# Cross attention added to 32 batches: slots of two adjacent rows, queries tile by tile

## The reference

```python
def _L0_xattn_ref(tgt, memory, Wq, Wk, Wv):      # tgt, memory: 32 x 512 x 512 f32
    NH = 16                                      # dk = 32
    q = (tgt @ Wq.T)...; k = (memory @ Wk.T)...; v = (memory @ Wv.T)...
    scores = jnp.einsum('bhqd,bhkd->bhqk', q, k) * scale
    probs = jax.nn.softmax(scores, axis=-1)
    att = jnp.einsum('bhqk,bhkd->bhqd', probs, v)
    tgt2 = att[0]
    return tgt + tgt2
```

## Time and profile before

| what | us |
|---|---|
| median of 3 runs | 198.37 (197.28 to 200.08) |
| the profiled execution | 198.03 |
| its span | 195.8 |
| PE busy | 129.3 (66%) |
| DVE busy | 103.1 (53%) |
| ACT busy | 92.6 (47%) |
| POOL busy | 84.0 (43%) |
| moved by DMA | 71.49 MB, mean 365 GB/s |

### The profile page before, as it was taken

The page is one execution under the profiler, slowest core; times in us unless marked ns, Lnnn a source line. Parts: engine busy times, 40 slices in busy tenths (PEclk is TensorE's granted clock), DMA queues, the critical chain, the costliest instruction groups (busy, mean ns, idle before and its releaser), DMA issues.

```text
span 195.8 us, 3210 instructions
## 1 busy us (share of the span) xinstructions
PE 129.3 (66%) x1213; PEld 95.6 (49%) x1213; DVE 103.1 (53%) x165; ACT 92.6 (47%) x221; POOL 84.0 (43%) x39
## 2 busy tenths in 40 slices
PE   6799999999898978989789897889720000000000
PEld 6788878878665655666556665556510000000000
DVE  0645565208454999759897598974279800000000
ACT  2624553202788958888598886988800000000000
POOL 1000000000000699999999999998059920000000
PEclk9999999999999999999999999999995555555555
DMA  6999999999998099999999999999999999999995
GB/s 208 331 397 387 385 387 386 387 386 385 388 386 305 24 338 343 340 340 270 390 396 389 387 403 409 403 408 403 406 393 388 408 408 409 409 409 408 408 388 210
DMA packets 40701, 71.49 MB, mean 365 GB/s; under 512 B 1264, under 2 KB 10480, under 8 KB 40688
## 3 DMA queue, kind: packets, MB, share of 16 engines
q1 hardware_dynamic: 40688, 71.31, 98.8%
HBM read 37.75 MB, written 33.55 MB: 364 GB/s over the span
## 4 chain that ended last, share of the span: by engine, by line
PE 38%; ACT 15%; DVE 11%; issue 5%; POOL 5%; DMA 3%; POOLq 2%; SPq 0%; ACTq 0%; DVEq 0%
PE bank L309 17%; ACT probs L420 9%; PE bank L367 7%; PE bank L333 6%; ACT probs_t L414 5%; PE bank L346 5%; POOL ring L272 5%; DVE neg_max L453 4%; DVE ring L492 3%; DMA x_first<-in_x_dram 3%; PE bank L322 3%; POOLq L55 2%; DVE x_first L492 2%; PE bank L357 1%; DVE att_t L463 1%
## 5 line engine op out<-in xcount | busy, mean ns | idle before, releaser
L272 POOL TENSOR_TENSOR ring<-ring,att 128x1024 f32 (+1 forms) x33 | 83.3, 2565 | 72.9 <-DVE att L476 72.9
L453 DVE TENSOR_REDUCE neg_max<-bank 128x1 f32<-128x512 f32 x64 | 41.6, 679 | 16.2 <-PE bank L333 16.2
L420 ACT ACTIVATE probs<-bank,neg_max 128x512 f32<-128x512 f32 x64 | 45.3, 709 | 8.4 <-DVE neg_max L453 8.3
L414 ACT COPY probs_t<-bank 128x512 f32<-128x512 f32 x64 | 37.8, 595 | 17.8 <-PE bank L367 17.7
L367 PE MATMUL bank<-ident,probs 128*128 128x128 f32 x256 | 39.0, 282 | 6.6 <-ACT probs L420 6.3
L367 PEld LDWEIGHTS bank<-ident,probs 128*128 128x128 f32 x256 | 27.4, 140 | 21.5 <-ACT probs L420 20.8
L333 PE MATMUL bank<-k_t,q_t 32*128 32x512 f32 x192 | 29.9, 424 | 0.0
L492 DVE TENSOR_TENSOR ring<-ring,bank 128x1024 f32<-128x1024 f32 (+1 forms) x16 | 23.2, 1478 | 0.6 <-DMA ring<-in_x_dram 0.6
L333 PEld LDWEIGHTS bank<-k_t,q_t 32*128 32x128 f32 x192 | 15.0, 183 | 7.1 <-issue 5.7
L346 PE MATMUL bank<-probs_t,v 128*32 128x128 f32 x512 | 17.3, 276 | 0.7 <-ACT probs_t L414 0.7
L346 PEld LDWEIGHTS bank<-probs_t,v 128*32 128x32 f32 x512 | 13.0, 109 | 4.0 <-ACT probs_t L414 4.0
(11 more groups left out here) (33 smaller groups left out, 72.1 us busy)
## 6 DMA issues: line engine op xcount, KB each, us to landing
ring<-in_x_dram SPq DMA_DIRECT2D x28, 1024.0 KB, 13.7
out_dram<-ring SPq DMA_DIRECT2D x21, 1024.0 KB, 13.4
out_dram<-ring SPq DMA_DIRECT2D x14, 512.0 KB, 6.1
x_first<-in_x_dram SPq DMA_DIRECT2D x4, 768.0 KB, 13.9
out_dram<-x_first SPq DMA_DIRECT2D x3, 1024.0 KB, 14.2
...
wk_raw<-in_L_xattn_Wk_dram SPq DMA_DIRECT2D x1, 1024.0 KB, 9.2
```

Of the source, the lines that this page charges most:

```text
L272: nc.gpsimd.tensor_tensor(xs, xs, a.unsqueeze(1).to_broadcast([P, BPG, a.shape[1]]), ALU.add).then_inc((tail_added if tail else added)[g], 1)
L414: nc.scalar.copy(probs_t[:, h % PT_SLOTS, :, :], bank[:, PT_BANK + h % 2, :].rearrange("p (t n) -> p t n", t=T)).then_inc(probs_t_ready, 1)
L420: nc.scalar.activation(probs[:, h % 2, :], bank[:, h % S_BANKS, :], ACT.Exp, bias=neg_max[:, h:h + 1], scale=1.0, accum_out=row_sum[:, h:h ...
L453: nc.vector.tensor_reduce(neg_max[:, h:h + 1], bank[:, h % S_BANKS, :], AX_X, ALU.max, negate=True).then_inc(max_ready, 1)
```

## The change

- Rows 2p and 2p + 1 of a half (256 rows) lie on partition p. A tile is now one of these rows of each partition: tiles 0 and 1 are the two rows of the first half, tiles 2 and 3 of the second. A slot holds two batches, both rows (1 MB, runs of 4 KB). There are 16 groups and 17 slots; `x_first` is gone. The order of the keys is changed likewise, which the sum over keys doesn't see.
- Queries are projected per tile, x as the stationary operand: x is turned, multiplied with wq (12 matmuls), scaled to `q_raw` by ACT, turned again and split by ACT and DVE. Tile 0's queries are made first, tile 1's during tile 0's heads, those of tiles 2 and 3 after the turn back of the tile before. The heads of tile 0 are interleaved with the products of keys and values, in an order written out for each engine.
- `heads(j)` issues no scores of the next tile; the first two pairs are issued ahead of it by `score_pair`. All tiles are turned back and normalised whole.
- Tiles 0 and 1 are added and stored by rows of slots (512 KB, rows of 2 KB), 9 groups by DVE and 7 by POOL, 1024 elements a partition each. The second half is added and stored by whole slots after tile 3, 11 by DVE and 5 by POOL, 2048 elements each.
- In `heads` DVE puts an add ahead of every maximum from head 0 on while any are left: eight in tile 1, five in tile 2, none in tile 3.
- SP loads slots when the operand that lies there is used up: slot 7 after the turns of wq, 8 and 9 after those of wk, 10 after those of wv, 11 and 12 after the keys, 13 to 16 after the last values.
- ACT's order in tile 0, not shown: exponents run up to three heads ahead of the copies, and `copy_transposed(0, h)` waits from h = 6 on until the group that used its place in `probs_t` is weighed.

```diff
-BPG = 4
+BPS = 2
+ROWS = 2
...
+    S_BANKS = 4
+    PT_BANK, BACK_BANK, ATT_T_BANK = 4, 6, 7
+    PT_SLOTS = 6
+    POOL_GROUPS = (1, 3, 5, 7, 10, 12, 14)
+    DVE_GROUPS = (0, 2, 4, 6, 8, 9, 11, 13, 15)
+    WHOLE_POOL_GROUPS = (2, 5, 8, 11, 14)
+    WHOLE_DVE_GROUPS = (0, 1, 3, 4, 6, 7, 9, 10, 12, 13, 15)
+    LAST_HALF = T // ROWS - 1
...
-    x_rows = x.rearrange("b (j p) d -> p j b d", p=P)
-    out_rows = out.rearrange("b (j p) d -> p j b d", p=P)
+    x_rows = x.rearrange("b (j p r) d -> p j b r d", p=P, r=ROWS)
+    out_rows = out.rearrange("b (j p r) d -> p j b r d", p=P, r=ROWS)
...
-        x_first = sb("x_first", [P, T, BPG, D])
...
+        WQ_RAW, WK_RAW, CTX_RAW, WV_RAW, WK_T, CTX_T, WV_T = 7, 8, 9, 10, 11, 13, 15
...
+        slots = sb("slots", [P, SLOTS, BPS, ROWS, D])
...
+        x0_q = sb("x0_q", [P, 2, C, 2, P], F32R)
...
+        att_rows = sb("att_rows", [P, ROWS, D])
+        att, q_raw = att_rows[:, 0, :], att_rows[:, 1, :]
...
+        JOBS = [("x0_t", 0, 0), ("wq_t", 0, 1), ("wq_t", 1, 2), ("wq_t", 2, 3), ("wq_t", 3, 4), ("q", 0, 5),
+                ("wk_t", 0, 6), ("ctx_t", 0, 7), ("q_t", 0, 0), ("ctx_t", 1, 1), ("ctx_t", 2, 2), ("ctx_t", 3, 3),
+                ("k_t", 0, 4), ("wk_t", 1, 5), ("k_t", 1, 6), ("wk_t", 2, 7), ("wk_t", 3, 4), ("wv_t", 0, 5),
+                ("k_t", 2, 6), ("wv_t", 1, 7), ("wv_t", 2, 7), ("k_t", 3, 6), ("wv_t", 3, 7),
+                ("x0_t", 1, 6), ("v", 0, 7), ("v", 1, 6), ("v", 2, 7), ("v", 3, 6),
+                ("q", 1, 6), ("q_t", 1, 0)]
+        for j in range(2, T):
...
+        def slot_of(J, g):
+            return g if J == 0 else (g - 1) % SLOTS
...
+            def load(J, g):
+                sp.dma_start(slots[:, slot_of(J, g), :, :, :], x_rows[:, J, 2 * g:2 * g + 2, :, :]).then_inc(
+                    loaded[J][g], 16)
+            def store_row(r, g):
+                sp.wait_ge(added[g], r + 1)
+                sp.dma_start(out_rows[:, 0, 2 * g:2 * g + 2, r, :], rows_of(0, g, r)).then_inc(stored[g], 16)
+            def store_slot(g):
+                sp.wait_ge(added[g], ROWS + 1)
+                sp.dma_start(out_rows[:, LAST_HALF, 2 * g:2 * g + 2, :, :],
+                             slots[:, slot_of(LAST_HALF, g), :, :, :]).then_inc(stored[g], 16)
+            def reload(g):
+                sp.wait_ge(stored[slot_of(LAST_HALF, g)], ROWS * 16)
+                load(LAST_HALF, g)
...
+            for g in range(1, GROUPS):
+                if g == WQ_RAW:
+                    sp.wait_ge(bank_filled, number["wq_t", C - 1] + 1)
+                if g == WK_RAW:
+                    sp.wait_ge(bank_filled, number["wk_t", C - 1] + 1)
+                if g == WV_RAW:
+                    sp.wait_ge(bank_filled, number["wv_t", C - 1] + 1)
+                if g == WK_T:
+                    sp.wait_ge(bank_filled, number["k_t", HG - 1] + 1)
+                if g == CTX_T:
+                    sp.wait_ge(bank_filled, number["v", T - 1] + 1)
                 load(0, g)
+            load(LAST_HALF, 0)
+            LAG = 3
+            for g in range(GROUPS):
+                store_row(0, g)
+            for g in range(GROUPS):
+                store_row(1, g)
+                if g >= LAG:
+                    reload(g - LAG + 1)
+            for g in range(GROUPS - LAG + 1, GROUPS):
+                reload(g)
+            for g in range(GROUPS):
+                store_slot(g)
+            for g in range(GROUPS):
+                sp.wait_ge(stored[g], (ROWS + 1) * 16)
...
+            for r in range(ROWS):
+                pool.wait_ge(att_ready, r + 1)
+                for g in POOL_GROUPS:
+                    pool.wait_ge(loaded[0][g], 16)
+                    xs = rows_of(0, g, r)
+                    nc.gpsimd.tensor_tensor(xs, xs, att.unsqueeze(1).to_broadcast([P, BPS, D]),
+                                            ALU.add).then_inc(added[g], 1)
+            pool.wait_ge(att_ready, T)
+            for g in WHOLE_POOL_GROUPS:
+                pool.wait_ge(loaded[LAST_HALF][g], 16)
+                xs = slots[:, slot_of(LAST_HALF, g), :, :, :].rearrange("p b r d -> p b (r d)")
+                nc.gpsimd.tensor_tensor(xs, xs, last_att.unsqueeze(1).to_broadcast([P, BPS, ROWS * D]),
+                                        ALU.add).then_inc(added[g], 1)
...
+            def score_group(g):
+                emptied(pe, "k_t", g)
+                if g > 0:
+                    pe.wait_ge(exp_ready, g * HPG)
+                scores(0, range(g * HPG, (g + 1) * HPG))
+            def score_pair(j, pair):
+                pe.wait_ge(exp_ready, j * HEADS + pair * PAIR - PAIR)
+                scores(j, range(pair * PAIR, (pair + 1) * PAIR))
+            def turn_probs(j, h):
+                pe.wait_ge(exp_ready, j * HEADS + h + 1)
+                if j * HEADS + h >= 2:
+                    pe.wait_ge(probs_t_ready, j * HEADS + h - 1)
+                for t in range(T):
+                    last = nc.tensor.transpose(bank[:, PT_BANK + h % 2, t * P:(t + 1) * P],
+                                               probs[:, h % 2, t * P:(t + 1) * P], ident[:, :])
+                last.then_inc(transposed, 1)
...
+            pe.wait_ge(x0_loaded, 16)
+            turn("x0_t", 0)
+            for i in range(C):
+                if i % 2 == 0:
+                    pe.wait_ge(wq_loaded[i // 2], 16)
+                turn("wq_t", i)
+            queries(0)
+            pe.wait_ge(wk_loaded, 16)
+            turn("wk_t", 0)
+            pe.wait_ge(ctx_loaded, 16)
+            turn("ctx_t", 0)
+            turn_queries(0)
+            for c in range(1, C):
+                turn("ctx_t", c)
+            keys(0)
+            turn("wk_t", 1)
+            keys(1)
+            turn("wk_t", 2)
+            emptied(pe, "ctx_t", C - 1)
+            score_group(0)
+            turn("wk_t", 3)
+            pe.wait_ge(wv_loaded, 16)
+            turn("wv_t", 0)
+            keys(2)
+            turn("wv_t", 1)
+            emptied(pe, "wk_t", 3)
+            turn_probs(0, 0)
+            emptied(pe, "wv_t", 0)
+            turn_probs(0, 1)
+            turn("wv_t", 2)
+            keys(3)
+            turn("wv_t", 3)
+            turn_probs(0, 2)
+            turn_probs(0, 3)
+            score_group(1)
+            pe.wait_ge(x0_loaded, 16)
+            turn("x0_t", 1)
+            values(0)
+            turn_probs(0, 4)
+            turn_probs(0, 5)
+            values(1)
+            values(2)
+            turn_probs(0, 6)
+            turn_probs(0, 7)
+            score_group(2)
+            values(3)
+            emptied(pe, "v", T - 1)
+            weigh_values(0, 0)
+            query_chunk(1, 0)
+            turn_probs(0, 8)
+            turn_probs(0, 9)
+            query_chunk(1, 1)
+            weigh_values(0, 1)
+            turn_probs(0, 10)
+            turn_probs(0, 11)
+            score_group(3)
+            query_chunk(1, 2)
+            query_chunk(1, 3)
+            turn_probs(0, 12)
+            turn_probs(0, 13)
+            weigh_values(0, 2)
+            turn_probs(0, 14)
+            turn_probs(0, 15)
+            turn_queries(1)
+            weigh_values(0, 3)
+            turn_back(0)
+            emptied(pe, "q_t", 1)
+            score_pair(1, 0)
+            score_pair(1, 1)
+            heads(1)
+            turn_back(1)
+            for j in range(2, T):
+                if j == 2:
+                    pe.wait_ge(loaded[LAST_HALF][0], 16)
+                turn("x0_t", j)
+                queries(j)
+                turn_queries(j)
+                emptied(pe, "q_t", j)
+                score_pair(j, 0)
+                score_pair(j, 1)
                 heads(j)
                 turn_back(j)
...
+            def normalize(j):
+                dve.wait_ge(att_back, j + 1)
+                dve.wait_ge(recip_ready, (j + 1) * HG)
+                if 0 < j < T - 1:
+                    dve.wait_ge(added[POOL_GROUPS[-1]], j)
+                to = att_rows[:, 1 if j == T - 1 else 0, :]
+                back = bank[:, ATT_T_BANK if j == T - 1 else BACK_BANK, :].rearrange("p (h d) -> p h d", d=DK)
+                inverse = recip[:, :].unsqueeze(2).to_broadcast([P, HEADS, DK])
+                nc.vector.tensor_tensor(to.rearrange("p (h d) -> p h d", d=DK), back, inverse,
                                         ALU.mult).then_inc(att_ready, 1)
                 nc.vector.tensor_tensor(back, back, inverse, ALU.mult).then_inc(att_ps_ready, 1)
+            def add(r, g):
+                dve.wait_ge(att_ps_ready, r + 1)
+                dve.wait_ge(loaded[0][g], 16)
                 if g == 0:
+                    dve.wait_ge(x0_loaded, 16)
+                xs = rows_of(0, g, r)
+                nc.vector.tensor_tensor(xs, xs, bank[:, BACK_BANK, :].unsqueeze(1).to_broadcast([P, BPS, D]),
+                                        ALU.add).then_inc(added[g], 1)
+            def add_whole(g):
+                dve.wait_ge(att_ps_ready, T)
```

(52 more changed lines are left out.)

522 lines of the change are left out of this document (196 added, 326 removed).

## The result

| | before | after |
|---|---|---|
| median of runs | 198.53 us (4 runs, 197.28 to 200.08) | 229.59 us (4 runs, 228.17 to 230.29) |
| profiled execution | 198.03 us, span 195.8 us | 230.29 us, span 228.5 us |
| mean granted clock | 0.873 | 0.803 |
| turn backs | tile 0 at 73.10 (its second half row), tile 3 at 142.76 (whole row) | whole rows: 70.73, 102.56, 143.54, 180.70 |

The changed kernel is slower by a factor of 1.1551, with a 95% interval of 1.1449 to 1.1654. The forecast was 223 with a range of 212 to 233. The time is inside the range, but outside the forecast's own range of 217 to 228, and it is what the rival "the clock falls" gave (about 230). Some executions of every kernel come out more than 1.5% above its fastest: medians and ranges here are of all executions, and ratios leave such executions out where there are enough others.

A forecast was written before the change was run, and what follows sets the result against it. Before, the attention chain set the first store and transfers the end; after, the chain plus held-back stores: T0 68.7 + tiles 31.4, 38.1, 33.7 + block 48.7 = span 220.6, about 223 us; range 212 to 233.

The forecast's parts named there:

- the clock falls: Rival, chance 0.25: PE's idle gaps in tiles 1 and 2 halve its clock, costing 2 to 5 us each; about 230.
- The last block: From the start of tile 3's turn back to the span's end, 16.8 MB of stores included: 48.7 us, upper bound 51.1.
- T0: Start of tile 0's turn back: 68.7 us, bounds 66 to 72, with 1.55 added for query chunks and a late maximum.
- queries(0) is over by then: Step ahead of tile 0's turn back: tile 0's query product is finished when ctx lands at 14.7 us.
- Tile 1: From tile 0's turn back to tile 1's: 31.4 us, with pairs of DVE add and maximum at 1.73 each.
- Tiles 2 and 3: From each turn back to the next: 38.1 us for tile 2, 33.7 for tile 3, with queries projected after the boundary.
- T1: Start of tile 1's turn back, forecast as T0 + 31.4.
- hidden better: Rival, chance 0.13: DVE pairs cost less or products run inside ACT's time; three tiles in 93, end 213.
- Not slower: Rival, chance 0.05: attention keeps 23.2 us a tile and transfers set the end; time 198 to 201.
- T3: Start of tile 3's turn back, forecast as T2 (tile 2's turn back) + 33.7.
- DMA's stops: DMA was to stand still three times: before tile 0's, tile 1's and tile 3's turn backs.
- the transfers ahead of T3: 54.5 MB at 400 GB/s, 136 us, counted as costing nothing because DMA stands still three times.

The follow-up runs named there:

- e1_fill: The changed kernel with PE's idle gaps filled by throw-away transposes of the identity, nothing else changed: 221.48 us, 1.1152 of the kernel before.
- e2_small_adds: The changed kernel with DVE's row adds of tiles 0 and 1 cut from 512 to 8 columns: 220.60 us, 1.1152 of the kernel before.
- e3_queries_early: The changed kernel with each next tile's queries, first two score pairs and first four maxima made ahead of the tile boundary: 222.02 us, 1.122 of the kernel before.
- e4: The changed kernel with the second half added and stored by rows, row 2 behind tile 2's turn back: 212.79 us, 1.0613 of the kernel before.

## Why the prediction was right, and where it was off

**The last block** was right in kind and to 0.9 us: 47.8 measured, 48.7 forecast. First add 2.03 behind the turn back, as forecast, and the issue at 4.34. At the mean of the windows from 186 and from 206, 404 GB/s, the stores take 41.5, so start and end together take 1.9 and not the 3.4 of the sum.

**T0** was forecast at 68.7; the kernel after had 70.73, e1_fill 69.19 and e2_small_adds 67.35. The step that failed is "queries(0) is over by then": in the kernel after the second part of wq came 1.03 us later than in e2, its turns took 1.35 and not 0.85, and the 12 weight loads of the product 4.38 and not 2.63, at a granted clock of 0.50 from 10 to 14 us. So PE reached the turns of ctx at 17.44 (15.97 in e1_fill). From the turn behind the product on (15.98, 14.50 and 12.66) the three take the same 54.7 us to T0. Of the 3.4 us between the first and the last, 1.0 is thus the later wq and 2.3 the clock. Without either the sum's allowance for waits (1.55 among them) was 1.4 too long.

**Tile 1** was 31.8 for 31.4. Pairs of add and maximum are 1.73 apart, as in rows 7, and e2_small_adds shows that they, not PE, set the pace of its first half: without them 4.0 less.

**Tiles 2 and 3** were 41.0 and 37.2 for 38.1 and 33.7. e1_fill has 38.0 and 33.5, and the steps inside agree too: head 8 of tile 2 was forecast to be turned 26.1 behind T1, and in e1_fill it is at 26.06 (126.64). So the dependency chain x0_t, product, q, scores, maximum was priced right, and e3_queries_early confirms its size from the other side: with the chain hidden, tile 3 takes 22.4. With the clock held up the three tiles take 102.9 for the 103.2 of the sum, so the rival "hidden better" (93) has fallen too.

**The term that was missing is the clock**, which the prediction had as a rival at 0.25. The rival's mechanism is what happened, its total (about 230) is what was measured, and its place was half right: it named the gaps of 4.1 and 3.5 us behind T1 and T0. In the trace PE is idle there for 4.24 and 4.65 us, and the clock is at 0.50 behind both. It did not name the gap ahead of queries(0), nor tile 3's, where waits of 1.84, 1.11, 1.66 and 2.29 us between short bursts went with it. Its prices were too high, for a product (2.65 more forecast, 1.5 and 1.8 measured) and for heads (0.9 each forecast; in tile 3 eight cost 3.7 together, 0.46 each). In tile 1, where it had put 2 to 5 us, the fall cost 0.4. That the total came out right is partly luck: prices too high for two tiles stood in for falls ahead of T0 and in tile 3 that it didn't have. The chance of 0.25 was the error: the stretches of before at 1.00 have only short gaps, so no row spoke for the clock staying up across gaps of 4 us, and yet the forecast was summed as if it did. The Trainium skill, page TensorE: Matmul & The Clock Gate, section HAM oscillation, says that a kernel whose PE idles between bursts loses the full rate again and again and pays for each return; here the trace agrees: the grant falls anew behind each of these gaps, and holding it up gained 8.1 us.

**"Not slower"**, the rival on the other side, had its point of decision at T3 no later than 149. The runs of the kernel before put it at 145.4 by a block of 50.4. With T3 at 180.7, or 172.1 without the clock, it never came near.

**DMA's stops** were to be three and were four. The one at 50 us is SP waiting for v 3 ahead of the last four loads (issued at 54.80 together). The prediction had named this gate among the things without cost, and it is: everything loaded there is long in place at T0.

**What the prediction did not see** lies behind its own answer. It counted the transfers ahead of T3 as free. They are in the kernel after; but they have a floor of their own, T1 + 108.3, which in the changed kernel would be at about 211 (102.56 + 108.3), 17.6 us under its span. e4 measured 16.8 for just this. With whole slots the floor decides once T3 is less than 60.5 behind T1 (108.3 less 47.8). And in the kernel after it is itself some 15 us over the span before (210.9 and 195.8), so whoever mends only the last block gets a little more than half back.
